# Spreading VectorE's rounding of the attention values over two pipeline steps

## The reference, cut to what matters

```
ln = layernorm(layernorm(x)) * w + b
q, k, v, qx = fp8(clip(ln / in_scale)) @ weights          # 16, 8, 8, 16 heads of 128
kx, vx      = ctx @ weights                               # 8 + 8 heads
q, k, qx, kx = layernorm of each head
core = softmax(q k^T / sqrt(128)) v ;  xout = softmax(qx kx^T / sqrt(128)) vx
cat  = concat(core, xout)
catq = fp8(bf16(clip(cat / smooth, -448, 448)))           # the rounding of the values
x    = x + tanh(g) * (catq @ wproj) * scale
```

## Time and profile before

| | |
|---|---|
| median of 3 runs | 453.41 us (452.15 to 453.7) |
| the profiled execution's own time | 453.45 us |
| its span in the profile | 451.7 us |
| busy in the span | PE 393.8 (87%), DVE 365.4 (81%), ACT 292.3 (65%), POOL 282.9 (63%) |
| last projection of the attention steps ends | near 324.8 us |

### The profile page before, as it was taken

How to read it: one execution, slowest core, us unless ns; L and a number is a source line. 1 busy time by engine, 2 the same in 40 slices (tenths; PEclk the granted TensorE clock), 3 DMA queues, 4 the chain that set the end, 5 groups by cost and what they waited for, 6 DMA issues and landing times.

```text
span 451.7 us, 11249 instructions
## 1 busy us (share of the span) xinstructions
PE 393.8 (87%) x3626; PEld 290.1 (64%) x3626; DVE 365.4 (81%) x836; ACT 292.3 (65%) x620; POOL 282.9 (63%) x379
## 2 busy tenths in 40 slices
PE   0677899999989989989998998998999496999960
PEld 0444567666757757656775675766687395899950
DVE  5967989999999999999999999999988761433337
ACT  3598888777767857767776775786963213666520
POOL 2079677875876778677687677855674740366640
PEclk9999999999999999999999999999988588999995
DMA  8950929999940000000000000000194213344317
GB/s 212 265 198 2 155 34 299 254 294 270 257 135 0 0 0 0 0 0 0 0 0 0 0 0 0 0 1 2 39 429 176 96 56 95 109 130 146 92 49 238
DMA packets 34621, 45.57 MB, mean 101 GB/s; under 512 B 2970, under 2 KB 32031, under 8 KB 33696
## 3 DMA queue, kind: packets, MB, share of 16 engines
q1 hardware_dynamic: 26368, 35.34, 26.4%
q0 software_dynamic: 6944, 9.46, 9.5%
q10 hardware_dynamic: 1280, 0.41, 0.4%
HBM read 28.21 MB, written 24.19 MB: 116 GB/s over the span
## 4 chain that ended last, share of the span: by engine, by line
PE 34%; DVE 31%; issue 14%; ACT 10%; POOL 6%; DMA 2%; ACTq 1%; POOLq 1%; SPq 0%; DVEq 0%
PE proj_ps L969 6%; DVE st L1378 6%; DVE yv L1405 3%; PE proj_ps L961 3%; PE out_ps L1031 3%; PE pv_ps L1021 3%; PE proj_ps L1137 3%; PE score_ps L998 3%; PE headT_ps L1137 3%; DVE ys L1344 2%; DVE reg L1389 2%; PE headT_ps L987 2%; DVE mx L1386 2%; DVE sm L1395 2%; ACT kT L744 2%
## 5 line engine op out<-in xcount | busy, mean ns | idle before, releaser
L969 PE MATMUL proj_ps<-arena 128*128 128x512 f16 x384 | 99.7, 382 | 3.0 <-DVE arena L1370 3.0
L1378 DVE BATCH_NORM_STATS2 st<-rot 128x6 f32<-128x256 f32 x192 | 72.4, 419 | 5.7 <-ACT rot L709 4.4
L571 POOL TENSOR_TENSOR rot<-rot,cw 128x512 f32<-128x512 f32 x64 | 67.3, 1072 | 2.5
L730 ACT ACTIVATE rot<-rot,cw 128x128 f32<-128x128 f32 x128 | 40.9, 391 | 32.7 <-POOL cw L565 32.7
L709 ACT ACTIVATE rot<-proj_ps 128x512 f32<-128x512 f32 x96 | 56.2, 585 | 8.1 <-PE proj_ps L969 6.5
L577 POOL TENSOR_TENSOR reg<-reg,rinv 128x512 f32<-128x512 f32 x32 | 33.5, 1047 | 35.3 <-DVE rinv L1398 35.3
L969 PEld LDWEIGHTS proj_ps<-arena 128*128 (+1 forms) x384 | 34.8, 98 | 29.4 <-issue 3.8
L641 POOL DMA_INDIRECT ybuf<-arena,bslot x31 | 30.6, 985 | 32.4 <-DVE bslot L1584 15.4
L961 PE MATMUL proj_ps<-arena 128*128 128x512 f16 x192 | 46.7, 379 | 0.6 <-POOL arena L527 0.6
L987 PE MATMUL headT_ps<-idf,rot 128*128 128x128 f32 x256 | 39.0, 275 | 8.3 <-ACT kT L744 8.3
L987 PEld LDWEIGHTS headT_ps<-idf,rot 128*128 128x128 f32 x256 | 30.0, 141 | 16.5 <-issue 9.9
(11 more groups left out here) (228 smaller groups left out, 874.1 us busy)
## 6 DMA issues: line engine op xcount, KB each, us to landing
zbuf<-fill SPq DMA_DIRECT2D x1, 16576.5 KB, 65.4
arena<-in_wffn SPq DMA_DIRECT2D x4, 1536.0 KB, 13.4
arena<-zbuf SPq DMA_DIRECT2D x30, 128.5 KB
wkv_stage<-in_wkvN SPq DMA_DIRECT2D x1, 2048.0 KB, 15.3
wp_sb<-in_wpT POOLq DMA_DIRECT2D x1, 2048.0 KB, 16.6
wp_sb<-ybuf SPq DMA_DIRECT2D x8, 256.0 KB, 5.5
xs<-in_x SPq DMA_DIRECT2D x2, 512.0 KB, 5.2
vv<-in_wqN POOLq DMA_DIRECT2D x1, 1024.0 KB, 12.4
```

Of the source, the lines that this page charges most:

```text
L571: gp.tensor_tensor(r, r, cw[:, 4 * i:4 * i + 4].unsqueeze(2).to_broadcast([P, 4, D]), ALU.mult)\
L730: ins = act.activation(r, r, ACT.Copy, scale=cw[:, h:h + 1])
L969: mm = pe.matmul(ps, lhs, w[kind][:, ch, 512 * b:512 * b + 512], start=(k == 0), stop=(k == 3))
L1378: ins = ve.bn_stats(st[:, 4 * i + h:4 * i + h + 2, :].rearrange("p h s -> p (h s)"), raw[c % 2][i][:, h * D:(h + 2) * D].rearrange("p (h d ...
```

## The change: what it does

1. The output product of unit n-4 moves, on TensorE, from behind `values(n-3)` to behind the first head transposes, so `project(2)` and `head_transposes(n-1, 0)` come ahead of it.
2. The two PSUM tensors of the values become one of two banks, and `over_smooth` is one instruction of 128x1024. It moves from behind `stats(n, 2)` to ahead of it.
3. The rounding of unit n-3 is split. Clip, abs and mag stay at the end of step n; big stands first in step n+1, and grid stands between the maximum and the subtraction of unit n-1 there. In the hardware loop grid waits for scores instead of the output product of two units before (the scores' count implies it).
4. At c = 1, clip, abs and mag of the values alternate with clip, abs and mag of the next tile's inputs, instead of preceding them.
5. In the tail, big of unit 28 stands first and its grid behind `rows_in(1)`.

No computation is added or left out. The diff, cut to its core:

```diff
-        pv_ps = [bank("pv_ps0"), bank("pv_ps1")]
+        pv_both = ctx.enter_context(nc.psum_tensor("pv_ps", [P, 1024], F32))
+        pv_ps = [pv_both[:, 0:512], pv_both[:, 512:1024]]
@@ TensorE step
                     values(n - 3, (c - 3) % NU)
-                if live(n, 4) and proj:
-                    output(n - 4, c, t - 1)
                 if proj:
                     project(t, c, 2)
...
                     head_transposes(n - 1, before, 0)
-                if live(n, 4) and not proj:
+                if live(n, 4):
                     output(n - 4, c, t - 1)
                 if proj:
                     project(t, c, 3)
@@ VectorE
             def over_smooth(w, u, y=yv):
                 ve.wait_ge(pv_done, w + 1)
-                for b in range(2):
-                    ins = ve.tensor_tensor(y3[:, :, b * S:(b + 1) * S], ...)
-                ins.then_inc(y_done, 1)
+                ve.tensor_tensor(y[:, :].rearrange("p (h b s) -> p b h s", b=2, s=S),
+                                 pv_both[:, :].rearrange("p (b h s) -> p b h s", b=2, s=S),
+                                 smi[:, 8 * u:8 * u + 8].unsqueeze(1).unsqueeze(3).to_broadcast([P, 2, 8, S]),
+                                 ALU.mult).then_inc(y_done, 1)
+            def values_big(w, y=yv):
+                ve.wait_ge(mag_done, w + 1)
+                ve.tensor_tensor(ys[:, :], y[:, :], ym[:, :], ALU.add).then_inc(big_done, 1)
+            def values_grid(w, u):
+                ve.wait_ge(big_done, w + 1)
+                if isinstance(w, int):
+                    ge(ve, op_done, w - 1)
+                else:
+                    ve.wait_ge(score_done, w + 3)
+                ve.tensor_tensor(catq[u % 2], ys[:, :], ym[:, :], ALU.subtract).then_inc(catq_done, 1)
@@ VectorE step
+                if live(n, 4):
+                    values_big(n - 4)
                 if proj:
                     stats(n, c, 0)
...
-                    softmax_in(n - 2, c % 2)
+                    softmax_max(n - 2)
+                if live(n, 4):
+                    values_grid(n - 4, c)
+                if attend:
+                    softmax_sub(n - 2, c % 2)
                 if proj:
                     stats(n, c, 1)
...
                     softmax_sum(n - 2, c % 2)
+                if live(n, 3):
+                    over_smooth(n - 3, (c - 3) % NU)
                 if proj:
                     stats(n, c, 2)
...
+                spread = c == 1 and live(n, -NU)
                 if live(n, 3):
-                    over_smooth(n - 3, (c - 3) % NU)
+                    values_clip(n - 3)
+                if spread:
+                    inputs_clip(t + 1)
                 if live(n, 3):
-                    quantise(n - 3, (c - 3) % NU)
-                if proj and c == 1 and live(n, -NU):
-                    inputs_magnitude(t + 1)
+                    values_abs(n - 3)
+                if spread:
+                    inputs_abs(t + 1)
+                if live(n, 3):
+                    values_mag(n - 3)
+                if spread:
+                    inputs_mag(t + 1)
                 if c == 3 and live(n, NU):
                     residual(t - 1)
@@ VectorE tail
+            values_big(last - 4)
             rows_in(1)
-            softmax_in(last - 2, 0)
+            values_grid(last - 4, 0)
+            softmax_max(last - 2)
+            softmax_sub(last - 2, 0)
```

More of the change, by code:

```diff
@@ L1328, in _, with inputs_clip, inputs_abs @@
                 fold_low(j)
-            def to_grid(y, q, sems, n, wait_free=None, by_pool=False):
-                clip, absolute, mag, big, grid = sems
-                ve.tensor_scalar(y, y, FP8_MAX, -FP8_MAX, ALU.min, ALU.max).then_inc(clip, 1)
-                ve.wait_ge(clip, n + 1)
-                ve.tensor_scalar(ya[:, :].bitcast(U16), y.bitcast(U16), 0x7FFF, None,
-                                 ALU.bitwise_and).then_inc(absolute, 1)
-                ve.wait_ge(absolute, n + 1)
-                ve.tensor_scalar(ym[:, :], ya[:, :], 128.0, 3.0, ALU.mult, ALU.max).then_inc(mag, 1)
-                if by_pool:
-                    return
-                ve.wait_ge(mag, n + 1)
-                ve.tensor_tensor(ys[:, :], y, ym[:, :], ALU.add).then_inc(big, 1)
-                ve.wait_ge(big, n + 1)
-                if wait_free:
-                    wait_free()
-                ve.tensor_tensor(q, ys[:, :], ym[:, :], ALU.subtract).then_inc(grid, 1)
-            def inputs_magnitude(T):
+            def inputs_clip(T):
                 ve.wait_ge(xin_done, T + 1)
                 ve.tensor_scalar(xin[:, :], xin[:, :], FP8_MAX, -FP8_MAX, ALU.min, ALU.max).then_inc(xclip_done, 1)
+            def inputs_abs(T):
                 ve.wait_ge(xclip_done, T + 1)
@@ L1356, in inputs_magnitude, with inputs_mag @@
                                  ALU.bitwise_and).then_inc(xabs_done, 1)
+            def inputs_mag(T):
                 ve.wait_ge(xabs_done, T + 1)
@@ L1413, in quantise, with values_abs, values_mag @@
+            def values_abs(w, y=yv):
+                ve.wait_ge(clip_done, w + 1)
+                ve.tensor_scalar(ya[:, :].bitcast(U16), y[:, :].bitcast(U16), 0x7FFF, None,
+                                 ALU.bitwise_and).then_inc(abs_done, 1)
+            def values_mag(w):
+                ve.wait_ge(abs_done, w + 1)
                 if isinstance(w, int) and w == NU * NT - 2:
                     ve.wait_ge(catq_done, w)
-                to_grid(y[:, :], catq[u % 2], (clip_done, abs_done, mag_done, big_done, catq_done), w,
-                        lambda: ge(ve, op_done, w - 1), by_pool)
+                ve.tensor_scalar(ym[:, :], ya[:, :], 128.0, 3.0, ALU.mult, ALU.max).then_inc(mag_done, 1)
@@ new lines, in quantise, with softmax_max, softmax_sub @@
+            def quantise(w, u, y=yv):
+                values_clip(w, y)
+                values_abs(w, y)
+                values_mag(w)
+                values_big(w, y)
+                values_grid(w, u)
+            def softmax_max(w):
+                ve.wait_ge(score_done, w + 1)
+                ve.tensor_reduce(mx[:, :], score_ps[:, :].rearrange("p (g t) -> p g t", t=S), AX.X,
+                                 ALU.max).then_inc(max_done, 1)
+            def softmax_sub(w, s):
+                ve.wait_ge(max_done, w + 1)
+                ge(ve, probn_done, w - 1)
+                ve.tensor_tensor(prob[s].rearrange("p (g t) -> p g t", t=S),
+                                 score_ps[:, :].rearrange("p (g t) -> p g t", t=S),
+                                 mx[:, :].unsqueeze(2).to_broadcast([P, 8, S]),
+                                 ALU.subtract).then_inc(sub_done, 1)
@@ L1611, in _ @@
             softmax_sum(last - 2, 0)
-            quantise(last - 3, 1, by_pool=True)
-            softmax_in(last - 1, 1)
+            values_clip(last - 3)
+            values_abs(last - 3)
+            values_mag(last - 3)
+            softmax_max(last - 1)
+            softmax_sub(last - 1, 1)
             route_best(0)
```

21 lines of the change are left out of this document (5 added, 16 removed).

## The result

The changed kernel takes 440.47 us, the median of 4 runs (439.2 to 441.95); the kernel before takes 453.12 in 4 runs beside it. In a second series of 6 and 11 runs the ratio was 0.974 (0.9699 to 0.9781). Some executions of every kernel come out a few per cent slower, with the core's clock lower: the ratios here leave them out, the medians and ranges hold them, and the profile of the kernel with the product early is of one, so only its period and its waits are used.

What follows compares the result with a forecast made beforehand. VectorE's list, laid end to end, was taken as the 37.38 us period, with TensorE's own list at 35.7. From 453.45 us, 8.9 came off in the loop and 0.5 was added in the tail: 445.0 us, range 441.8 to 450.5.

Steps and rivals of the forecast that it cites:

- The bound: Attention loop: TensorE's waits come from VectorE's lateness; a faster VectorE brings at most 1.7 us a period.
- The alternation, and the way it pays: VectorE at c = 1: inputs' abs and mag run ahead of the norm banks, saving 1.44 us; alternating saves another 0.6.
- Dependent neighbours: VectorE's list: independent neighbours and over_smooth as one instruction save 0.4 us a step.
- Grid, moved: VectorE, between maximum and subtraction: grid waits for a norm bank, 0.6 us a step, leaving 0.3 to 0.4 a period.
- The sum over the loop: TensorE's eight stalls in the loop: 7.0 us back from five full ones and 1.9 from three others, 8.9 together.
- the bound with nothing left over: Most the loop could give: 5 x 1.66 + 2.35, and 0.1 for each of seven tiles, 11.4 us.
- The tail: Attention's tail: grid of unit 28 meets the norm banks of unit 31, 0 to 1.02 us, taken as 0.5 slower.
- Plus or minus 1.5 us, taken as 0: Tail, 335 to 338 us: a different wait could shift TensorE's low-clock stretch by plus or minus 1.5 us, taken as 0.
- Output product, later: TensorE, behind `project(2)` and four transposes: `catq` should be just in time, cost 0, with grid's wait as risk.
- Half of it is given back: Rival, chance 0.13: grid's waits exceed the slack at c = 0 and c = 1, giving 449.4 us.
- nothing to measure: Rival, chance 0.05: VectorE's slack and grid's waits cancel, 453.4 us.
- Grid behind the norm banks in every step: Slower rival, chance 0.12: grid waits 1.02 us in each of 28 steps, giving 457 us.

Runs made afterwards that it cites:

- the kernel with the product early: Changed kernel with the output product back ahead of `project(2)`: 450.3 us, ratio 0.9843 to the kernel before.
- The kernel with less TensorE work: Changed kernel without the low-weight matmuls of the values' last bank at c = 0 and c = 1: 437.44 us in one run.
- the one with more VectorE work: Changed kernel with one more independent VectorE maximum of 128x512 behind big in each step: 458.09 us in one run.
- the kernel with the rounding together: Changed kernel with big and grid back at the end of the values' own step: 446.49 us, then 440.25 us beside the changed kernel's 440.99.
- the alternation-alone kernel: Kernel before with only the inputs' clip, abs and mag alternating with the values': 450.98 us, ratio 0.9895.
- with over_smooth behind: Changed kernel with over_smooth, still one instruction, back behind the third statistics: 444.35 us in one run, 448.38 us when run again.

## Why the prediction was right, and where it was wrong

The mechanism and the direction were right, and the time came out below the range. Two terms of the sum were mis-sized. The loop was to give back 8.9 of 11.4 us, because some of grid's waits were to be left over, and gave 11.5; the tail was to cost 0.5 and gave 1.4.

**The bound.** Right. TensorE's waits were VectorE's lateness; once VectorE's list was the shorter one they were gone, and the period came down by 1.73, the "1.7 us a period" named as the most that could be had. The starts of the scores in both traces show the eight waits going one by one: 1.64 to 1.66 us at each of the five full ones, and 0.79, 0.76 and 1.33 at the other three. The kernel with less TensorE work (34.96) shows the new bound.

**The alternation, and the way it pays.** Right in size: the six operations now take 2.05 us from start to start (188.87 to 190.92, the statistics not counted), against 4.09 for the same six before, 1.38 for the first three and 2.71 from 196.35 to 199.06; the difference is the forecast 1.44 + 0.6. By itself it is worth 1.31 us a period.

**Dependent neighbours.** Right: big to statistics is 0.61 (190.92 to 191.53), maximum to grid 0.59. Clip and clip of two unrelated tiles follow at 0.33, clip and its own abs at 0.45 (197.54 to 197.99 in this trace). The section of the Trainium skill that the prediction set against this term ("VectorE: DVE Perf Modes", The DRAIN you can't avoid) also says that a next operation that is not held starts earlier. The prediction left that out, and the trace agrees with it. Over_smooth as one instruction was put at 1.11 to 1.13 to the next and measured 1.09 (195.78 to 196.87).

**VectorE's list.** 33.7 us was forecast, 33.1 measured. The over_smooth term gives 4 x 0.04 of the difference. Another 0.34 are three intervals that were longer in the period of before than in its other steps, and that the forecast kept in the list: reciprocal to statistics 0.26 for 0.12 (at 210.85), maximum to subtraction 0.80 for 0.70 (at 217.63), and big to grid 0.82 for 0.72 (at 224.00). And 0.12 came at c = 3, where the mag now has the independent residual behind it (0.34 for 0.46). Less than 0.1 is left.

**Grid, moved: the step that failed.** "I take 0.6" for each step, and "What is left, I put at 0.3 to 0.4 a period". Measured: 0.15, 0.17, 0.23 and 0.57, together 1.1 instead of 2.4, on a list 0.6 shorter than forecast. Waits and list together stay 1.5 us below TensorE's, so nothing is left over. Nor did any grid of the loop run at 0.69, as was expected for some; they took 0.84 to 1.34. The reason given for the high value ("a VectorE with slack arrives late") was right in its first half only: arriving late inside the first bank shortens the wait, since just the rest of that bank is to be sat out. The mechanism itself, a wait for the first bank only, is as described in this kernel, though not in the one with more VectorE work. The rule of the Trainium skill ("SBUF — State Buffer", Who interferes with whom) agrees with the 0.84 to 1.26 us of grid and the 2.48 of the norm banks. The abs at 1.15, which the prediction also counts to it, reads one SBUF tile; the sentence on two inputs does not cover it.

**The sum over the loop.** "I take 1.4 of each back: 7.0" and 1.9 for the rest made 8.9; the trace has 11.5, the 11.4 of "the bound with nothing left over" within 0.1. This is 2.6 of the 5.0 us between 445.0 and the profiled 440.0. The bound had been worked out and should have been the likeliest value. TensorE stands only for what VectorE is late by, so a list that is short enough brings the whole 1.66 and not a share of it; 2.0 us of slack against 2.4 of waits left nearly nothing to be late by.

**The tail.** Forecast +0.5 for grid of unit 28; it took 1.24 us (317.65) beside norm banks of 2.81, 0.55 of it waiting, and the tail of the kernel with the rounding together is 27.08 against 27.94, 0.9 shorter: inside the bounds of 0 to 1.02. (That kernel is no faster for it, since its loop had taken 1.2 us longer: 247.4 against 246.2.) Yet the tail became 1.4 shorter, and the low-clock stretch did not come. How much of it the clock gave is not shown: the alternation-alone kernel's 28.06 without the fall puts it at 0.7 to 1.3 us, an estimate from one trace. "Plus or minus 1.5 us, taken as 0" held the size and had no sign. It was also left out of the range, whose low end is the full bound with an unchanged tail; with it the low end would have been 453.45 - 11.4 - 1.5 = 440.6. Together with grid the tail explains 1.9 of the 5.0 us. The remaining 0.5 lies ahead of the loop and behind the attention, and is less than the 2.7 us between this kernel's own runs.

**Output product, later.** "Cost 0" was right, and too modest: with the split it is worth 0.48 us a period, and 3.1 where over_smooth is not early either (38.84 against 35.7).

**The rivals.** "Half of it is given back" and "nothing to measure" fell with the period of 35.65. "Grid behind the norm banks in every step" did not come, but its mechanism exists: with 2.4 us more on VectorE's list grid met the second bank in three of four steps and big the first bank in the fourth, the waits grew from 1.1 to 2.8 us a period, and the whole gain was gone (458.09). What protected the changed kernel is that its grids fall due inside the first bank, and that its list leaves room for what they wait. The slower outcome that the rivals lacked is the ring: product behind grid, `project(2)` behind the product, grid behind the statistics of `project(2)`. It was two edits away (38.84), and the change holds both remedies.

**Still open**: what decides the clock in the tail, and how much of the tail's 1.4 us it gave.

## What to carry to other kernels

Where two engines are both near 96% busy, write down each one's own list and compare: once the shorter one is below the other by more than its own waits, take the whole bound as the forecast, and nothing beyond it for any further edit of that engine. Those waits are no constant, though: they hang on the moment at which an instruction falls due, and more work in front of it can double them. When half of a chain is moved into the next step, follow the ring through all engines from its result back to itself before trusting the busy shares: in it a kernel can lose 4% with no engine full. And read the granted clock in a tail too: in the kernel before, a wait of 0.8 us stood ahead of 12 us at reduced clock.

## What the hardware showed that was not expected

- A VectorE instruction with two SBUF sources that falls due during GpSimd's first norm bank gets in between the two, although GpSimd's second one follows at once: grid 0.84 to 1.26 us, the pair 2.04 to 2.48. Due just past the first bank it waits for the second (1.54, the pair at 2.04).
- Such waits are set by the moment: with 4 x 0.6 us of added work that itself reads one source only they grew from 1.1 to 2.8 us a period and cost 2.6; in the kernel without the alternation 2.2 us of them cost 0.06.
- The attention's tail ran at a granted clock of 1.00 up to 336 us in four traces (the changed kernel and the one with the rounding together, twice each) and fell to 0.50 to 0.65 in both of the kernel before and both with over_smooth behind; the tails of these four were 0.9 to 4.5 us longer than the changed kernel's.
